# A fused gated-expert and low-rank feed-forward kernel: last weight load cut into 112 rows and 1 row, expert numbers read earlier on TensorE, weight split at another place in VectorE's order

## The reference

```python
# first step, h = layernorm(x), expert e of the row
g = silu(h @ W[e].T);  u = h @ W[e].T;  y = (g * u) @ Wd[e].T
x = x + tanh(g_xattn) * y
# second step, h = layernorm(x)
base   = h @ W_base + b_base
shared = (h @ A_s) @ B_s
gates  = softmax(h @ W_router + b_router)        # 6 experts, the 2 largest are kept
routed = sum over e of gate[e] * (h @ A_r[e]) @ B_r[e]
x = x + tanh(g_ffn) * (base + shared + routed)
```

## Time and profile before

| | us |
|---|---|
| median of three runs | 223.96 |
| lowest and highest of them | 223.73, 225.19 |
| the profiled execution | 224.34 |
| its span in the trace | 222.6 |
| mean granted clock of TensorE over the span | 0.978 |

### The profile page before, as it was taken

The page is one execution under the profiler, slowest core; times in us unless marked ns, Lnnn a source line. Parts: engine busy times, 40 slices in busy tenths (PEclk is TensorE's granted clock), DMA queues, the critical chain, the costliest instruction groups (busy, mean ns, idle before and its releaser), DMA issues.

```text
span 222.6 us, 3748 instructions
## 1 busy us (share of the span) xinstructions
PE 200.0 (90%) x1095; PEld 153.7 (69%) x1096; DVE 151.0 (68%) x416; ACT 108.9 (49%) x200; POOL 107.8 (48%) x164
## 2 busy tenths in 40 slices
PE   0599798699999985999999999999999999999970
PEld 0345586588888873777787888877877777777750
DVE  4886968846566751766887765566787887885560
ACT  4554242543444732546445446463676675775410
POOL 4787764734343000011366644313377677767241
PEclk9999999799999999699999999999999999999997
DMA  4967015659976695022255552322378888899932
GB/s 122 377 213 280 4 49 140 156 129 177 224 191 160 36 56 46 0 49 47 47 188 183 184 151 97 94 47 50 86 104 121 134 129 131 123 113 146 141 53 94
DMA packets 41855, 27.12 MB, mean 122 GB/s; under 512 B 35137, under 2 KB 35137, under 8 KB 41842
## 3 DMA queue, kind: packets, MB, share of 16 engines
q1 hardware_dynamic: 36336, 12.60, 30.1%
q0 software_dynamic: 4816, 12.85, 25.6%
q10 hardware_dynamic: 690, 1.52, 2.4%
HBM read 10.71 MB, written 7.86 MB: 83 GB/s over the span
## 4 chain that ended last, share of the span: by engine, by line
PE 66%; DMA 12%; DVE 9%; issue 5%; ACT 3%; POOL 1%; SPq 1%; POOLq 1%
PE y_ps L595 13%; PE z_ps L595 13%; PE y_ps L600 6%; PE z_ps L600 6%; DMA hT_half<-h_split 5%; DMA ct_stage<-ct 5%; PE ffn_a L605 4%; PE ffn_b L605 4%; PE actT_ps L614 4%; DMA h2T<-h_split 3%; PE ffn_b L609 2%; PE ffn_a L609 2%; PE z_ps L605 2%; PE y_ps L605 2%; DVE ct_split L813 2%
## 5 line engine op out<-in xcount | busy, mean ns | idle before, releaser
L595 PE MATMUL z_ps<-ct_split,hT 128*128 x144 | 40.2, 424 | 2.2 <-issue 2.2
L595 PE MATMUL y_ps<-ct_split,actT 128*128 x152 | 38.6, 396 | 0.0
L595 PEld LDWEIGHTS z_ps<-ct_split,hT 128*128 128x128 f32 x144 | 27.2, 197 | 9.0 <-issue 3.9
L595 PEld LDWEIGHTS y_ps<-ct_split,actT 128*128 128x128 f32 x152 | 28.5, 188 | 6.8 <-ACT actT L447 0.2
L318 POOL TENSOR_SCALAR var_eps<-stats 128x1 f32<-128x1 f32 x19 | 3.6, 190 | 54.0 <-DVE stats L894 53.8
L447 ACT ACTIVATE actT<-actT_ps 128x512 fp32r<-128x512 f32 x19 | 11.4, 598 | 37.3 <-PE actT_ps L614 37.3
L396 POOL DMA_INDIRECT out<-scaled,row_index x14 | 22.4, 1601 | 9.4 <-ACT scaled L496 4.8
L327 POOL DMA_INDIRECT xg<-x_rows,row_index x19 | 21.7, 1140 | 5.9 <-issue 2.6
L917 DVE TENSOR_TENSOR act<-z_ps,silu 128x512 f32<-128x512 f32 x18 | 12.4, 688 | 17.6 <-ACT silu L443 16.9
L898 DVE TENSOR_SCALAR h<-xg,stats,rstd 128x512 f32<-128x512 f32 x19 | 10.4, 546 | 17.3 <-POOL rstd L321 17.3
L600 PE MATMUL y_ps<-ct_split,actT 128*128 x76 | 20.8, 395 | 0.0
(11 more groups left out here) (176 smaller groups left out, 418.8 us busy)
## 6 DMA issues: line engine op xcount, KB each, us to landing
ct_stage<-ct SPq DMA_DIRECT2D x4, 1024.0 KB, 8.1
ct_stage<-w_ffn ACTq DMA_DIRECT2D x4, 315.0 KB, 3.1
xg<-x_rows,row_index POOLq DMA_INDIRECT x19, 4.3
hT_half<-h_split SPq DMA_TRANSPOSE x16
out<-xg,row_index POOLq DMA_INDIRECT x16, 2.7
h2T<-h_split SPq DMA_TRANSPOSE x16, 3.3
ct_stage<-w_up ACTq DMA_DIRECT2D x1, 226.0 KB
out<-scaled,row_index POOLq DMA_INDIRECT x14
```

What stands on the lines that cost most here:

```text
L595: nc.tensor.matmul(ps, lhs[:, 0, at], rhs(part), start=(k == 0 and part == 0), stop=False)
```

## The change

Three things are edited.

1. The load of `w_up` is issued as two: rows 0 to 111, and row 112. Both count on the same semaphore, and its reader waits for 32 in place of 16.
2. TensorE's loop body begins one product later: the first z of the loop (item 3) is written ahead of it, and a turn for item q is y(q-1), transpose of q, z(q+1). The order of the products is the same. The two expert numbers of a turn are read at its head, ahead of the waits of y(q-1). As the squares' matmul stands between the two loops, it now comes after z(9), before it came ahead of z(9).
3. On VectorE the weights' part moves from the end of an iteration to the place between `item_aggregate(q+3)` and `item_norm(q+3)`. `w_scales` is cut in two, `w_exponent` in iteration 9 and the rest in iteration 10, and the split of the weights begins in iteration 11 in place of 10 on both engines (`W_SPLIT_AT`); `w_up` is split in iteration 15. The register load of an extra's target goes to the same place, ahead of the weights' part.

```diff
-        W_SPLIT_AT = W_SCALE_AT + 1
+        W_SPLIT_AT = W_SCALE_AT + 2
...
-                    act_e.wait_ge(up_loaded, 16)
+                    act_e.wait_ge(up_loaded, 32)
...
-                    act_e.dma_start(up_stage, w_up).then_inc(up_loaded, 16)
+                    act_e.dma_start(up_stage[0:LORA], w_up[0:LORA]).then_inc(up_loaded, 16)
+                    act_e.dma_start(up_stage[LORA:], w_up[LORA:]).then_inc(up_loaded, 16)
...
-            def item(q, slot):
-                product_z(q, slot)
-                product_y(q - 1)
+            product_z(DMA_FROM, DMA_FROM % 2, key_of(DMA_FROM))
+
+            def item(q, next_slot):
+                key, next_key = key_of(q - 1), key_of(q + 1)
+                product_y(q - 1, key)
                 transpose_act(q)
+                product_z(q + 1, next_slot, next_key)
...
+            def w_exponent():
 
                 dve.wait_ge(w_totalled, 1)
                 after(cp(w_total[:], squares_ps[:, 0:1]))
                 after(ts(w_power[:, 0:1], w_total[:].bitcast(I32), 23, None, ALU.logical_shift_right))
                 after(ts(w_power[:, 1:2], w_power[:, 0:1], 1.0, None, ALU.add))
                 after(ts(w_power[:, 2:3], w_power[:, 1:2], 1, None, ALU.logical_shift_right))
+
+            def w_scales():
+
                 ts(w_power[:, S_INVERSE:S_INVERSE + 1], w_power[:, 2:3],
...
+                target = target_of(q - 1) if EXTRA_AT <= q - 1 < EXTRA_AT + EXTRAS else q - 1
+                if q == W_SCALE_AT:
+                    w_exponent()
+                if q == W_SCALE_AT + 1:
+                    w_scales()
+                if W_SPLIT_AT <= q < W_SPLIT_AT + KC:
+                    w_lo(q - W_SPLIT_AT)
                 if q + 3 < ITEMS:
                     item_norm(q + 3)
                     dve.wait_ge(h_ready, q + 4)
-                product_of(q - 1)
+                product_of(q - 1, target)
                 if q >= ITEMS - 2:
                     h2_lo(q + 2 - ITEMS)
                 actT_lo(q)
-                if q == W_SCALE_AT:
-                    w_scales()
-                if W_SPLIT_AT <= q < W_SPLIT_AT + KC:
-                    w_lo(q - W_SPLIT_AT)
```

More of the change, by code:

```diff
@@ L634, in transpose_h, with product_z @@
                 transpose_chunks(hT_ps, h).then_inc(hT_done, 1)
-            def product_z(q, slot):
-                key = key_of(q)
+            def product_z(q, slot, key):
                 pe.wait_ge(hT_ready, q - DMA_FROM + 1)
@@ L640, in product_z, with product_y @@
                 expert_lo(z_ps, hTs[slot], key).then_inc(z_done, 1)
-            def product_y(q, key=None, bank_used=True, between=None):
-                if key is None:
-                    key = key_of(q)
+            def product_y(q, key, bank_used=True, between=None):
                 if bank_used:
@@ L728, in _ @@
             expert_lo(z_ps, hT, key_2).then_inc(z_done, 1)
-            product_y(1)
+            product_y(1, key_1)
             transpose_act(2)
-            def item(q, slot):
-                product_z(q, slot)
-                product_y(q - 1)
+            product_z(DMA_FROM, DMA_FROM % 2, key_of(DMA_FROM))
+            def item(q, next_slot):
+                key, next_key = key_of(q - 1), key_of(q + 1)
+                product_y(q - 1, key)
                 transpose_act(q)
+                product_z(q + 1, next_slot, next_key)
             with pe.Fori(DMA_FROM, W_SQUARE_AT + 1, 2) as q:
                 for turn in range(2):
-                    item(q + turn, (DMA_FROM + turn) % 2)
+                    item(q + turn, (DMA_FROM + turn + 1) % 2)
             pe.wait_ge(w_squared, 1)
@@ L744, in _ @@
                 for turn in range(2):
-                    item(q + turn, (W_SQUARE_AT + 1 + turn) % 2)
-            item(ITEMS - 2, (ITEMS - 2) % 2)
-            item(ITEMS - 1, (ITEMS - 1) % 2)
+                    item(q + turn, (W_SQUARE_AT + turn) % 2)
+            item(ITEMS - 2, (ITEMS - 1) % 2)
+            last_key, key = key_of(ITEMS - 1), key_of(ITEMS - 2)
+            product_y(ITEMS - 2, key)
+            transpose_act(ITEMS - 1)
             pe.wait_ge(w_hi_ready, KC + 1)
@@ L754, in _ @@
             ffn_lo(0).then_inc(ffn_done, 1)
-            product_y(ITEMS - 1)
+            product_y(ITEMS - 1, last_key)
             def tile(l, turn, landing, bank_used=True):
@@ L943, in w_lo @@
                     w_split[:, bass.ds(k * 2 * WN, WN)], ALU.mult, ALU.subtract).then_inc(w_lo_ready, 1)
-            def w_scales():
+            def w_exponent():
                 dve.wait_ge(w_totalled, 1)
@@ L977, in _, with product_of @@
             actT_lo(0)
-            def product_of(q):
+            def product_of(q, target):
                 if EXTRA_AT <= q < EXTRA_AT + EXTRAS:
                     dve.wait_ge(x2_ready, q)
-                    add_product(q, target_of(q))
-                else:
-                    add_product(q, q)
+                add_product(q, target)
             item_stats(3)
```

## The result

The changed kernel takes 216.53 us (median of 4 runs, 215.95 to 217.11) against 224.5 (4 runs, 223.73 to 225.19): a ratio of 0.9646, 95% interval 0.9597 to 0.9695, faster. The forecast was 217.1 us, a ratio of 0.969 to its 223.96. The median lies in the range. By the medians 8.0 us were won, not 6.9; half of the difference of 1.1 us is that the kernel before came out at 224.5 here and the forecast started from 223.96.

A forecast was written before the change was run, and what follows sets the result against it. TensorE, busy 90% of the span, was taken as the bound. Losses of 1.05 + 3.11 + 3.05 = 7.21 us, less 0.3 for the squares, gave 6.9 us: 217.1 us from 223.96, range 216.0 to 219.4.

The forecast's parts named there:

- Part 1: w_up load in 112 rows and 1: lands within 3.1 us, removing the 3.11 us stall before z(10) and its after-effect.
- The clock's 1.55 us: TensorE at z(10), behind the stall: the granted clock of 0.50 costs 1.55 of the 3.05 us, and this goes.
- Rival A: w_up load: 112 rows don't spread, item 10's transpose still lands at 86.0, only 1.7 us won, 222.3 us; chance 0.04.
- Part 2, squares: TensorE at z(9): with the squares' matmul behind z(9) the 1.05 us loss goes, less 0.3 for the matmuls.
- Part 2, reads: Head of TensorE's turn: two expert number reads cost about 1.0 us but are hidden, at most 0.2 us an item.
- Rival D: Head of TensorE's turn: two loads decide y's start, making the kernel slower, 232 us with no sequencer lead; chance 0.02.
- lead of 1.75 us: TensorE's sequencer in item 9: it reached the load at 81.2, and y(8) began at 82.95; called the worst item.
- Part 3: VectorE's order: moving the weights' part and target load into its wait for GpSimd's root removes 1.50 us by z(14).
- The hold on GpSimd: w_lo beside GpSimd's root delays the normalisation of iterations 11 to 14, 0.8 us taken, covered by 0.90 us of slack.
- rival B: VectorE stays the bound in iterations 10 to 14: the 1.50 us stay, 5.4 us won, 218.6 us; chance 0.12.
- Rival C: Second step: a late transpose stops TensorE, one stall of 1 to 2 us, 218.1 to 219.1 us; chance 0.05.
- this is all that can be won among these items: TensorE from z(8) to z(14): the losses sum to 7.21 us, with no idle time in the stretch behind.

The follow-up runs named there:

- Experiment 2: The changed kernel with w_up as one load of 113 rows again: 221.18 us, ratio 0.9883 to the kernel before.
- experiment 3: The changed kernel with TensorE's order as before, the squares' matmul ahead of z(9): 217.7 us, ratio 0.9704.
- experiment 8: The changed kernel with four expert number reads in place of two at the head of every TensorE turn: 219.06 us, ratio 0.9818.
- experiment 1: The kernel before with only the w_up load split into 112 rows and 1: 219.63 us against 224.05, ratio 0.9816.
- experiment 4: The changed kernel with VectorE's order as before and the weights' split from iteration 10: 217.12 us, ratio 0.9704.
- experiment 9: The changed kernel with eight matmuls in TensorE's wait for item 2's act, and w_lo moved behind the addition: 215.14 us, ratio 0.9645.
- experiment 7: The changed kernel run again unaltered, as a repeat: 215.34 us over 6 runs, ratio 0.9645.
- experiments 5 and 10: The changed kernel with eight matmuls in TensorE's wait for item 2's act, then its repeat: 215.13 and 215.18 us, ratios 0.9633 and 0.964.

## Why the prediction was right, and where it was not

**Part 1** held. One load of 113 rows kept item 10's transpose from landing for 10.7 us; in 112 rows and 1 the load is over in 1.3 us. The load's time was mis-sized (9.9 us, not 8.6), which changes nothing in the sum. Experiment 2 isolates it: 3.60 us of stall and 1.56 of clock behind it. The clock's 1.55 us was taken from the earlier trace rows and is confirmed. Rival A is out. The rule by which I said that 112 rows would spread (the Trainium skill, DMA: Bandwidth & Descriptors, section on why a DMA increments its semaphore by 16) gives 1, 3 and 16 engines for 113, 111 and 112 rows. The three loads agree in their order, and the first two in the ratio of three (25 against 73 to 76 GB/s); no view here shows which engines the packets ran on.

**Part 2, squares:** forecast 1.05 less 0.3, measured 1.05 less 0.20 between the two profiled executions and 0.88 in experiment 3.

**Part 2, reads:** the second read is free, as forecast. Rival D's price appears with four reads (experiment 8); three were not tried. The lead of 1.75 us on which I argued against it was read in one item; the turns' first item has less, which experiment 8 shows and my working did not.

**Part 3** was right in cause and in sum, with one term mis-sized. I split the 3.05 us of z(10) to z(14) into 1.55 for the clock and 1.50 for VectorE's round. Alone, the clock costs 1.57 (experiment 2) and VectorE's order with the late reads 2.40 (experiment 1): 3.97, not 3.05. In the kernel before they lay over one another, and the intervals show where: z(10) to z(11) lost 2.02 us there (97.22 - 89.19 less 6.01), while the two causes alone lose 1.56 (experiment 2) and 1.29 (experiment 1) in it, 2.85 together; the next two intervals lose nearly the same in the kernel before and in experiment 1, 1.02 and 1.09. That a slow z(10) gave VectorE time to get through the scales is the likely reading. So by the z starts experiment 1 gained 3.73 us (7.21 - 3.48), not the 4.66 of its theory. Its median came out 4.4 us lower all the same; the clock in z(3), low in the profiled execution before and at 1.00 in that of experiment 1, is enough to hide the miss. Of the 2.40 us, reading the expert numbers early takes off 1.06 (experiment 4: 1.34 left); moving VectorE's part takes off all of it (experiment 3: 0.01). I named the one cause and not that the other nearly doubles it. The sum of the prediction did not depend on this split: 3.05 was read off as a whole, and all of it went.

**The hold on GpSimd** came, but smaller than priced. In iterations 12 to 14 its first step takes 0.69, 0.77 and 0.77 us against 0.19 in experiment 9, in iteration 11 the second takes 0.98 against 0.55: a delay of 0.4 to 0.6 us, where the prediction took 0.8. VectorE's slack covered it, and rival B is out.

**Rival C** is out in these executions: TensorE stays busy all the time in the stretches set side by side above. Behind them stands one wait for a transpose of `h2_split` in each profile, 0.25 us before (20 us ahead of the end) and 0.42 us after (12 us ahead of it). From its first matmul to the end of the span the second step took 222.6 - 146.61 = 75.99 us and takes 214.2 - 138.06 = 76.14, so it gave back 0.15 us. The forecast had its first matmul at 139.7; it comes at 138.06.

**What failed** is the sentence "this is all that can be won among these items". The prediction's timeline began at z(7), and the low clock in z(3) was in the same trace 26 us earlier. It made the profiled execution before 1.33 us longer than the one after, and that is nearly all of 8.39 against 6.9. It is no clear gain of the change: the changed kernel shows it too, in 4 of 10 runs by the mean clock. Of the 28 runs of the kernel before that were made beside the experiments, 20 have a mean clock of 0.975 to 0.979 and eight 0.981 to 0.988. If the lower group is the one with the low z(3), it comes more often before than after. But only four of those eight are also the fastest of their comparison (222.2 to 222.5 us), and the first four runs of the changed kernel don't divide by time (215.95 and 216.84 us at 0.990, 216.21 and 217.11 at 0.985 and 0.984), so this is a hint and no more. Whether it matters that z(3) starts with less "issue" in the new order (0.41 us before) was not tried, and stays open; it does not decide it alone, as experiment 1 has 0.45 us there with the clock at 1.00, and experiment 7's profiled execution has none and the low clock.

The best version measured is that of experiments 5 and 10, the change with eight matmuls in the gap: 215.13 and 215.18 us. Its median is 0.2 us under the changed kernel's in the same comparison (215.34), which the intervals don't tell apart; its highest run is 215.53 against 216.24.

## What to carry to other kernels

A small DMA whose row count is not a multiple of 16 can cost more than a large one, because other transfers may wait with it: here 226 KB in 113 rows took 9.9 us and held a transpose for 10.7. Look for a flat floor of low bandwidth under a transfer that lands late, and cut the rows to a multiple of 16 and a rest. Work that an engine must do somewhere belongs in the wait that it has anyway, here VectorE's wait for GpSimd, and register reads ahead of the waits. When two losses lie in the same items, undo each alone before giving either a price: one may be hiding the other.

## What the runs showed of the hardware

- The row count of a DMA set the time of about the same 226 KB: 9.9 us in 113 rows (a floor of 27 GB/s in the view), 4.0 us in 111 and 2 (a floor of 70), 1.3 us in 112 and 1. Beside the 113-row load the transposes and the load together moved 46 to 96 GB/s (from 79.3 us on), with a DMA share of 0.90 over 80 to 89 us; alone the transposes reach 284 to 300.
- The granted clock of TensorE fell to 0.50 behind a wait of 2.03 us in one profiled execution of the changed kernel and stayed at 1.00 in the other, at a price of 1.3 us in the interval z(3) to z(4) (7.58 against 6.26 us) and about 1.0 us in the time within experiment 7. With the wait filled by matmuls no mean clock of 12 runs was under 0.989.
- TensorE's sequencer hid two register reads in a row at the head of a 6 us item; four cost 0.3 to 0.6 us in every second item and nothing in the others.
- GpSimd's first step on a 128x1 tile took 0.69 to 0.77 us beside VectorE's w_lo (0.87 us, two inputs in SBUF) and 0.19 without it.
